# GpSimd's two row scatters of a step placed behind the bias, the values and the first power

## The reference

```python
x = x + tanh(g_xattn) * attention(ctx, ctx, layernorm(x)) @ w_out.T + b_out   # bias is inside the gate
def ffn(x, Wg, W1, b1, W2, b2):
    logits = x @ Wg;  gates = softmax(logits)
    idx1 = argmax(gates);  idx2 = argmax(logits without idx1)
    w1, w2 = gate1 / (gate1 + gate2), gate2 / (gate1 + gate2)
    pos1 = running count of idx1 before this position
    pos2 = running count of idx2, behind all of the first choices
    xe[idx, pos] += x                              # rows of each expert, 2048 at most
    ye = gelu(xe @ W1 + b1) @ W2 + b2
    return ye[idx1, pos1] * w1 + ye[idx2, pos2] * w2
x = x + tanh(g_ffn) * ffn(layernorm(x), ...)
```

## Time and profile before

| | |
|---|---|
| median of 3 runs | 435.59 us |
| the profiled execution's own time | 435.74 us |
| its span in the profile | 433.9 us |
| busy: PE, DVE, ACT, POOL | 321.6, 280.0, 215.5, 214.1 us |
| TensorE clock granted in the attention stage | 1.00 of full speed |

### The profile page before, as it was taken

One profiled execution on the slowest core, in us unless ns is written; L12 is line 12 of the kernel. 1 busy time (PEld: TensorE's weight loads), 2 busy tenths in 40 slices (PEclk: granted clock), 3 DMA queues, 4 the chain that ended last, 5 costly groups with the idle time before them and its releaser, 6 DMA issues.

```text
span 433.9 us, 13799 instructions
## 1 busy us (share of the span) xinstructions
PE 321.6 (74%) x4010; PEld 258.0 (59%) x4011; DVE 280.0 (65%) x1104; ACT 215.5 (50%) x644; POOL 214.1 (49%) x352
## 2 busy tenths in 40 slices
PE   1488987877887787787640299999999999999100
PEld 0245655555554554555430299999999998999000
DVE  4758987787788778766567135555554554454397
ACT  1368865666666656664410164555555554555000
POOL 4323456756666675655575044555555545555100
PEclk9999999999999999999965599999999999999655
DMA  6943322211211210000011212112222221121494
GB/s 170 303 123 100 100 87 76 75 45 68 76 61 53 74 50 17 26 27 20 30 38 53 75 50 61 56 61 60 61 64 60 58 67 52 58 61 32 121 326 133
DMA packets 46476, 33.91 MB, mean 78 GB/s; under 512 B 5046, under 2 KB 41304, under 8 KB 46432
## 3 DMA queue, kind: packets, MB, share of 16 engines
q1 hardware_dynamic: 41504, 24.65, 20.1%
q0 software_dynamic: 4352, 8.43, 5.6%
q10 hardware_dynamic: 576, 0.26, 0.2%
HBM read 18.02 MB, written 15.83 MB: 78 GB/s over the span
## 4 chain that ended last, share of the span: by engine, by line
PE 33%; issue 21%; POOL 15%; DVE 7%; ACT 6%; DMA 5%; SPq 2%; DVEq 1%; another core or an unknown queue 1%; POOLq 0%; ACTq 0%
PE main_scores L648 14%; PE main_scores L662 13%; POOL expert_rows L422 8%; DMA choice_rows<-y_s,dest 2%; DVE x_all L860 2%; ACT probs L501 2%; POOL rstd L449 2%; ACT qT L494 2%; DVE x_all L858 2%; PE max_scores L639 2%; POOL rstd L442 1%; POOL values L438 1%; POOL x_all L429 1%; DMA yc<-choice_rows 1%; PE main_scores L581 1%
## 5 line engine op out<-in xcount | busy, mean ns | idle before, releaser
L462 POOL DMA_INDIRECT choice_rows<-y_s,dest x72 | 80.4, 1116 | 89.9 <-DVE y_s L840 65.5
L519 ACT ACTIVATE hT<-main_scores,ex_cur 128x128 f32<-128x128 f32 x288 | 82.1, 368 | 77.1 <-PE main_scores L648 66.2
L718 DVE TENSOR_REDUCE negmax<-max_scores 128x8 bf16<-128x1024 f32 x64 | 77.9, 1217 | 33.5 <-remote 19.8
L501 ACT ACTIVATE probs<-main_scores 128x1024 f32<-128x1024 f32 x64 | 62.0, 1021 | 45.3 <-issue 42.8
L648 PE MATMUL main_scores<-xtT,ex_cur 128*128 128x128 f32 x576 | 81.8, 286 | 3.0 <-DVE xtT L835 1.9
L662 PE MATMUL main_scores<-w_sb,hT 128*128 x576 | 80.3, 282 | 0.4 <-ACT hT L519 0.4
L648 PEld LDWEIGHTS main_scores<-xtT,ex_cur 128*128 128x128 f32 x576 | 71.4, 195 | 9.3 <-issue 3.9
L422 POOL DMA_INDIRECT expert_rows<-xrow,slot_i x64 | 64.2, 1003 | 16.8 <-issue 16.1
L662 PEld LDWEIGHTS main_scores<-w_sb,hT 128*128 128x128 f32 x576 | 69.8, 191 | 1.8 <-issue 0.6
L830 DVE COPY ex_cur<-ex_sb 128x644 f32 x72 | 35.8, 497 | 51.0 <-issue 45.5
L622 PE MATMUL mixed<-probs,values 128*32 128x128 f32 x1024 | 43.8, 281 | 1.6 <-issue 0.2
(11 more groups left out here) (130 smaller groups left out, 480.7 us busy)
## 6 DMA issues: line engine op xcount, KB each, us to landing
xt<-expert_rows SPq DMA_DIRECT2D x72, 64.5 KB
choice_rows<-zeros SPq DMA_DIRECT2D x16, 256.0 KB
yc<-choice_rows SPq DMA_DIRECT2D x16, 256.0 KB, 4.7
ex_sb<-in_L_ffn_W_dram SPq DMA_DIRECT2D x4, 512.0 KB, 4.7
w_sb<-in_L_ffn_W_dram SPq DMA_DIRECT2D x4, 512.0 KB, 4.4
out_dram<-x_all SPq DMA_DIRECT2D x8, 256.0 KB, 3.4
x_all<-in_x_dram SPq DMA_DIRECT2D x5, 384.0 KB, 6.4
ctx_all<-in_ctx_dram SPq DMA_DIRECT2D x5, 384.0 KB, 6.6
```

What stands on the lines that cost most here:

```text
L462: nc.gpsimd.indirect_dma_start(y_dram, bass.IndirectOffsetOnAxis(ap=dest[:, v, :], axis=0), y_s[:, v, :], None, bounds_check=last_row, oob ...
L501: nc.scalar.activation(probs[:, b % 2, 2 * g:2 * g + 2, :].rearrange("p g k -> p (g k)"), E_ALL[:, 1024 * g:1024 * g + 1024], ACT.Exp, sca ...
L519: last = nc.scalar.activation(hT[:, v % 2, c, :], H_BANK[v % 2][:, c * P:c * P + P], ACT.Gelu, bias=ex_cur[:, v, FF + D + c:FF + D + c + 1])
L718: V.tensor_reduce(negmax[:, m % 3, 2 * h:2 * h + 2, 0:J], S_ALL[:, :].rearrange("p (g j k) -> p g j k", g=2, j=J), AX.X, ALU.max, negate=T ...
```

## The change

In GpSimd's step the block of d, three waits and two indirect DMAs, is cut from the head and put behind the block of n. No instruction is added or removed, and no wait is changed.

```diff
             def step(t, n, x, a, m, b, p, q, c, w, r, k, d):
-                if d is not None:
-                    pool.wait_ge(slot_done, at(d, 1, 1))
-                    pool.wait_ge(ids_done, at(d, 1, 1))
-                    pool.wait_ge(xn2_ready, at(d, 1, 1))
-                    for i in range(2):
-                        nc.gpsimd.indirect_dma_start(
-                            xs_dram, bass.IndirectOffsetOnAxis(ap=slot_i[:, d % NX, i:i + 1], axis=0),
-                            xrow[:, d % NX, i, :], None).then_inc(row_out[d % NX], 16)
                 if x is not None:
...
                 if n is not None:
                     pool.wait_ge(ln1_var, at(n, 1, 1))
                     nc.gpsimd.tensor_tensor(rstd1[:, n % 2:n % 2 + 1], ve1[:, n % 2:n % 2 + 1], neg_half[:, :],
                                             ALU.pow).then_inc(ln1_rstd, 1)
+                if d is not None:
+                    pool.wait_ge(slot_done, at(d, 1, 1))
+                    pool.wait_ge(ids_done, at(d, 1, 1))
+                    pool.wait_ge(xn2_ready, at(d, 1, 1))
+                    for i in range(2):
+                        nc.gpsimd.indirect_dma_start(
+                            xs_dram, bass.IndirectOffsetOnAxis(ap=slot_i[:, d % NX, i:i + 1], axis=0),
+                            xrow[:, d % NX, i, :], None).then_inc(row_out[d % NX], 16)
                 if c is not None:
```

## The result

The changed kernel takes 457.55 us (median of 4 runs, 454.61 to 462.05) against 435.7 us for the kernel before beside it: 1.050 times as long, 95% interval 1.046 to 1.054. The slowest of the four runs is left out of that ratio. The forecast was 435.4 us with a range of 415 to 450, so both the time and its class were missed. The profiled execution took 457.65 us, 21.9 more than that of before.

A forecast was written before the change was run, and what follows sets the result against it. Scatters holding TensorE's signals were taken to bound each step at 6.33 us. New steps of 6.25 us save 1.7 over 21 steps, steps 31 to 34 add 1.4: 435.74 becomes 435.4 us, range 415 to 450.

The forecast's parts named there:

- What bounds the kernel: Attention stage: a pair of scatters holds TensorE's completion signals until some 0.6 us behind it, in a loop of 6.33 us.
- The terms of the new loop: Steps 10 to 30, maximum(0) to maximum(0): 2.19 + 0.16 + 0.23 + 0.75 + 1.36 + 0.96 + h, 6.25 us.
- the hold h: Wait from the end of the second scatter to maximum(0): taken as 0.60 us, bounds 0 to 0.71.
- The cover of the second power: Second power moves behind the scatters, done 4.05 us behind ve1, read by xrow at 5.65: cover of 1.6 us.
- Steps 31 to 34: Four steps whose scatters now stand behind the copies of the values: 0.36 us longer each, +1.4 us.
- The sum: Whole kernel: 435.74 - 1.7 (steps 10 to 30) + 1.4 (steps 31 to 34) = 435.4 us.
- The counts are held: Rival: held counts delay VectorE's second half, steps of 8.0 us; 448 us if every third, 454 if every second; chance 0.27.
- Nothing is caught: Rival: the moved scatters hold no signal that is waited for; steps of 5.42 us, 417 us in all; chance 0.28.
- The bound is unmoved: Rival: the idle time has nothing to do with scatters; steps stay at 6.33 us, time at 435.7 us; chance 0.04.
- same: Class of outcome: time within 1% of the kernel before, from the forecast (0.41) and the unmoved bound (0.04); chance 0.45.

The follow-up runs named there:

- e1: The kernel before with all 64 scatters issued behind step 41, from 32 buffers in place of 8; 491.81 us (one run).
- e2: As e1, but with two GpSimd memsets of 1152 columns where the scatters had been; 498.12 us (one run).
- e5: The changed kernel with fourteen useless products heading TensorE's steps 10 to 31, waiting only for the exponent's first half; 441.44 us, 1.012 of the kernel before.
- e9: The kernel before with the same fourteen useless products at the head of TensorE's step as in e5; 435.22 us, 1.002 of the kernel before.
- e3: The changed kernel with twenty useless products heading TensorE's steps with scatters, waiting for the whole exponent; 447.87 us, 1.023 of the kernel before.
- e7: The kernel before with one scatter left at the head of the step and the other behind the bias; 413.76 us (one run).
- e10: The kernel of e7 again, timed; 414.82 us, 0.953 of the kernel before.
- e12: The kernel before with scatter 0 moved behind the bias and scatter 1 behind the first power; 413.55 us, 0.950 of the kernel before.

## Why the prediction was wrong, point by point

**What bounds the kernel: right.** That the scatters hold TensorE's signals was an inference from rows 1 and 2; e1 shows it (5.35 us a step in place of 6.33), and e2 rules out that a busy GpSimd is enough. The Trainium skill (SBUF — State Buffer, "Who interferes with whom") says that TensorE and ScalarE never wait on anyone. Of the memory's ports that may hold; here scatters make ScalarE and VectorE wait for TensorE (a step of 6.33 us with them, of 5.35 without), and the runs decide.

**The terms of the new loop: right where the clock is full, but for the hold.** Behind a long step 6.27 us were measured, 6.25 forecast, with the first scatter 3.34 behind maximum(0) (3.33 forecast), xrow at 0.57 us and a release 0.62 behind the pair. In steps that follow one another at full clock everything up to the pair's end is the same, but the release comes later: in e5 the pair ends at 125.27 and maximum(0) starts at 126.08, 0.81 behind it, and 0.78 to 0.86 in all steps from 11 to 29. So the hold h was taken 0.2 us too short (0.60; its upper bound was 0.71), and the step is 6.46. The cover of the second power held as well (1.6 us, as forecast: done at 127.83, read at 129.41). Steps 31 to 34: in e5 rsum goes from 190.35 in step 30 to 214.64 in step 34, in e9 from 188.37 to 211.17, +1.5 us against +1.4 forecast.

**The sum: wrong.** "6.25 us ... over 21 steps -1.7 us" is the step that failed: I multiplied one step by 21. The 22 steps from 10 to 31 came out 18.8 us longer instead. Two things were missing.

First, one held step changes the next. The pair holds the products' signal, so ScalarE copies oS late and TensorE starts its next step late (1.50 to 1.59 us of standing ahead of L556 in its steps at full clock, where before it was 0.37). More of its instructions then lie inside the pair, and the hold behind the pair is 0.8 us and not 0.6; that the one is the reason of the other is argued, not shown. maximum(1) waits 0.47 us for the late maxima too, but the scatters follow ve1, ahead of it, so this wait is not in the loop. The difference of 6.46 to 6.33 is 0.13 x 20 = 2.6 us. And step 30 isn't one of the 21: it has no ve1 to wait for, its pair starts 0.6 us earlier and catches the maxima, 1.5 us in e5. Both make the 1.0% between e5 and e9, with the forecast steps 31 to 34.

Second, the margin and the clock. Behind a held step the main scores start late (L581 at 129.09 in the step of 127.73, 1.36 behind maximum(0) and not 0.27) and end 2.7 us behind maximum(0), the maxima behind them 2.95, or 0.6 and 0.4 ahead of the pair at 3.35. That was the whole margin, and it was computable: the rival on the counts worked with just such a delay of 1.20 us, but for the counts alone. And TensorE stands for 1.5 to 2.4 us in one piece, where in the kernel before its longest wait was 0.60 us in nearly every step (ahead of the maxima's L549). The granted clock then fell to 0.50 (113.20 to 119.90), and 0.95 us more on L581 used up the margin. The main scores and the maxima end inside the pair, and maximum(1), with all that hangs on it, waits for the pair's end: 9.4 us. Which waits make the clock fall isn't settled. Of the nine falls to half between 57 and 214 us, eight came inside a wait of TensorE of 1.44 us or more or at most 1.7 behind it; but three of eleven such waits had none, among them the longest (2.41 us ahead of 128.06, full grant from 128.1 to 134.1), and the first half grant, at 62 us, had only waits of 0.33 and 0.82 us ahead of it. With these waits filled, in e3 and e5, it didn't fall at all up to 200 us. That it is the clock which makes the steps long is shown by e5. The Trainium skill (TensorE: Matmul & The Clock Gate, "HAM oscillation — how this bites in real kernels") describes kernels whose TensorE loses its full clock in the waits between short bursts of work and starts each burst slow. For the most part the trace agrees, with the eight falls of nine and the three exceptions above, and this was the rule to weigh against the change.

I looked at TensorE only as the engine that is waited for. What a wait of TensorE does to its own speed was in no term and no rival.

**The rivals.** *Nothing is caught* (417 us): wrong for a pair, though its steps of 5.4 us are what e7 and e10 to e12 reach. *The counts are held* (448 to 454 us): it had the right size and the right sign to look for (steps above 8 us among those of 6, time above 440), with a chance of 0.27. That its size fits is luck, since its mechanism is not what happened: rsum stands behind maximum(1) in VectorE's list, and it is maximum(1) that waited, for the maxima. *The bound is unmoved*: excluded by e1.

**The chances.** 0.45 for "same" rested on the idea that one hold per step is exchanged for another of the same length. The rows were right; what could go wrong at the edge of a cover of 0.6 us wasn't priced.

From step 32 on the changed kernel lost another 4.3 us (the 3.1 left of 21.9, and 1.2 by which its step 10 had started earlier). There the clock was lower too: 0.77 in the 25.5 us from 214.48 on and 0.52 in the 35 us behind those, in place of 0.95 and 0.59. In e5, which has its products of no use up to step 31 only, step 32 comes at 198.76 and 239.4 us follow it, against 238.9 in the kernel before and 243.2 in the changed one, with a clock of 0.90 in the first 25.5. So most of these 4.3 us went with the clock as well, by one execution of each.

## What to carry to other kernels

Don't issue two indirect DMAs of GpSimd in a row beside a TensorE that works in many small instructions: 0.8 us or more between them, with other work of GpSimd in it, was worth 5% here (0.950 to 0.953 of the time), at each of three placements. (Whether it is the work or the pause that counts wasn't tried.) When a move keeps the length of a loop, look at what now ends just ahead of the moved piece, and how far ahead: a margin that one slower group can use up is a cliff, and a step beyond it took 9.0 us here in place of 6.3. Look at the first and last steps by themselves: where a wait ahead of the moved piece is gone, the margin is another one. And read a new long wait of TensorE as a risk to its own clock; a few products of no use in the wait are a cheap test of it, and they cost nothing in the kernel before.

## What the runs showed that was not expected

- A single scatter holds TensorE's signals for about 0.4 us behind its end, and of those that an engine stood waiting for none was more than some 0.5 us late; a pair with 0.30 us between its scatters holds them for up to 2.2 (109.83, the end of the products, to 111.99). How long the pause has to be was not tried; 0.81 us (e7 and e10) is enough.
- Whether a signal is held goes by how many matmul instructions end in a time: 16 of 128 columns in 0.89 us are held (1.84 us of wait in place of 0.67), 4 of 512 columns in 0.86 us are not (0.64 both ways), and 8 slow ones in f32, 1.8 us a round, are not either (1.56 both ways).
- e7 and e10 leave the bound to VectorE's list: 5.33 us a step, of which VectorE is busy for 5.23, and e12 nearly so (5.36). The next gain would have to come from there.
